# First attention: the third product of the turned scores folded into the second, with its operands built on ScalarE and VectorE

## The reference, cut to what matters

```python
q = (x @ Wq.T).reshape(B, T, NH, hd).transpose(0, 2, 1, 3)   # B=8 T=256 NH=16 hd=16
...
att = jnp.einsum('bhtd,bhsd->bhts', q, k) / jnp.sqrt(jnp.asarray(hd, x.dtype))
att = att + mask                      # causal
w = jax.nn.softmax(att, axis=-1)
z = jnp.einsum('bhts,bhsd->bhtd', w, v)
...
x = x + _layernorm(_L0_attn_ref(_layernorm(x, axis=-1), L0_attn_Wq, L0_attn_Wk, L0_attn_Wv, L0_attn_Wo), axis=-1)
```

## Time and profile before

| | |
|---|---|
| time, median of 3 runs | 1016.86 us (1005.52 to 1017.29) |
| the profiled execution's own time | 1014.95 us |
| its span in the trace | 1013.2 us |
| mean granted TensorE clock | 0.888 |
| PE busy | 853.5 us (84%), 6846 matmuls |
| PEld busy | 720.0 us (71%) |
| DVE busy | 741.6 us (73%) |
| ACT busy | 394.2 us (39%) |
| POOL busy | 441.6 us (44%) |

### The profile page before, as it was taken

How to read it: one execution, slowest core, us unless ns; L and a number is a source line. 1 busy time by engine, 2 the same in 40 slices (tenths; PEclk the granted TensorE clock), 3 DMA queues, 4 the chain that set the end, 5 groups by cost and what they waited for, 6 DMA issues and landing times. The chain is left out here.

```text
span 1013.2 us, 18850 instructions
## 1 busy us (share of the span) xinstructions
PE 853.5 (84%) x6846; PEld 720.0 (71%) x6846; DVE 741.6 (73%) x1561; ACT 394.2 (39%) x760; POOL 441.6 (44%) x582
## 2 busy tenths in 40 slices
PE   5899898897759877788888689999999989899973
PEld 4677777775648666677777568887878878788763
DVE  5678887876457653896666577888868777999894
ACT  2234333342323263333333254554455553333320
POOL 3123333322332237777775654666643213333332
PEclk9899999997669897899999977887778779999986
DMA  7000000000000037999987532211110000000001
GB/s 249 2 1 13 12 12 2 12 13 12 12 10 1 22 116 225 289 283 313 303 267 225 161 99 82 60 52 47 47 36 1 0 1 1 1 1 22 21 1 42
DMA packets 58315, 77.69 MB, mean 77 GB/s; under 512 B 9698, under 2 KB 50925, under 8 KB 58232
## 3 DMA queue, kind: packets, MB, share of 16 engines
q1 hardware_dynamic: 30968, 40.92, 12.8%
q0 software_dynamic: 9856, 18.92, 6.6%
q10 hardware_dynamic: 17408, 16.78, 4.8%
HBM read 61.88 MB, written 23.07 MB: 84 GB/s over the span
## 5 line engine op out<-in xcount | busy, mean ns | idle before, releaser
L516 POOL DMA_INDIRECT work<-xnd,rows_at x128 | 132.8, 1038 | 49.5 <-issue 33.2
L935 PE MATMUL ZO<-parts 128*128 128x256 f32 x288 | 90.6, 315 | 24.5 <-DVE parts L1523 7.2
L442 POOL TENSOR_SCALAR_AFFINE_SELECT work<-work 128x256 f32<-128x256 f32 x128 | 53.8, 444 | 128.4 <-ACT work L648 128.4
L433 POOL TENSOR_SCALAR veps<-mv 128x2 f32<-128x2 f32 x64 | 18.7, 292 | 193.3 <-DVE mv L1484 193.0
L1899 DVE TENSOR_TENSOR work<-work,S 64x256 f32<-64x256 f32 x128 | 54.2, 424 | 59.9 <-ACT work L774 55.8
L648 ACT ACTIVATE work<-S 128x768 f32<-128x768 f32 x64 | 52.0, 812 | 103.3 <-PE S L1008 103.3
L936 PE MATMUL ZO<-parts 128*128 128x256 f32 x288 | 84.9, 295 | 0.0
L937 PE MATMUL ZO<-parts 128*128 128x256 f32 x288 | 84.8, 294 | 0.0
L935 PEld LDWEIGHTS ZO<-parts 128*128 128x128 f32 x288 | 57.9, 201 | 33.1 <-issue 14.4
L935 PE MATMUL S<-xr,parts 128*128 128x512 f32 x192 | 79.2, 413 | 0.8 <-issue 0.8
L615 POOL TENSOR_TENSOR parts<-work,parts 128x512 fp32r<-128x512 f32 x32 | 44.1, 1378 | 80.3 <-ACT parts L891 80.3
(11 more groups left out here) (316 smaller groups left out, 2477.3 us busy)
## 6 DMA issues: line engine op xcount, KB each, us to landing
yd<-work ACTq DMA_DIRECT2D x64, 256.0 KB
raw<-in_experts SPq DMA_DIRECT2D x74, 192.0 KB
work<-in_experts SPq DMA_DIRECT2D x36, 192.0 KB
lg_all<-in_experts SPq DMA_DIRECT2D x18, 192.0 KB
raw<-in_ffn SPq DMA_DIRECT2D x2, 1536.0 KB, 7.4
xnd<-attn_w SPq DMA_DIRECT2D x8, 256.0 KB, 2.1
shd<-work SPq DMA_DIRECT2D x8, 256.0 KB, 2.4
work<-xnd,rows_at POOLq DMA_INDIRECT x128
```

Source lines behind the costliest of these rows:

```text
L442: last = pool.affine_select(out=diagonal, in_=diagonal, compare_op=ALU.is_ge, fill=0.0, base=0, pattern=[[0, 2], [1, P]], channel_multipli ...
L516: pool.indirect_dma_start(xg[:, i % RING, b, :], None, xnd[:], bass.IndirectOffsetOnAxis(ap=rows_at[:, 2 * i + b:2 * i + b + 1], axis=0), ...
L935: pe.matmul(dst, a(0), b(0), start=start, stop=False, skip_group_check=True)
```

## The change

Two of the three products become one. The key's low part needs only 16 of the 32 rows of a strip; the other 16 rows are now used for the selector of the maxima. So the second product's operands are `kx0`, which holds the key's low part in the upper 16 rows and the selector in the lower ones, and `qx0`, which holds `qm0` in the upper and the maxima's rows in the lower ones. A step has 8 turned matmuls instead of 12. To build the operands:

- ScalarE makes a third copy for each group, `khm`: the key times `upper` (1 in upper rows, 0 in lower) plus a negated selector. It stands ahead of the signal `a_q`.
- VectorE's second instruction in `key_copies` subtracts `khm` from the masked key; it is a scalar_tensor_tensor instead of a tensor_tensor.
- `spread_maxima` writes two copies of 32 elements each into `nmx` (zeros elsewhere) instead of one of 224.
- `maxima_low` has a second instruction, which waits for the first and forms `qx0` of group 0; a new `maxima_rows` forms groups 1 to 3 in one instruction of 768 elements, behind `key_copies(i+1, 1)`. `a_nm` is signalled twice in a round, and steps 0 and 2 of the turned scores wait for it.
- A few small instructions at the program's start build the masks.

```diff
             def query_copies(b, g):
                 act.wait_ge(s["a_qk"], 4 * b + g + 1)
                 act.activation(qh0, O[:, 0:T], ACT.Copy)
-                act.activation(kh0[:, b % 2, g, :], O[:, T:2 * T], ACT.Copy).then_inc(s["a_q"], 1)
+                act.activation(kh0[:, b % 2, g, :], O[:, T:2 * T], ACT.Copy)
+                act.activation(khm, O[:, T:2 * T], ACT.Identity, scale=upper[:, 0:1], bias=neg_pick[:, 0, g:g + 1]
+                               ).then_inc(s["a_q"], 1)
...
-                    side = (kh0, kl0)[k][rows, b % 2, g, half * P:(half + 1) * P] if k < 2 else                         bc(selc[rows, 2 * u + r:2 * u + r + 1], [32, P])
-                    top = (qm0[rows, b % 2, g, :] if k < 2 else nm0[rows, :])[:, half * P:T]
+                    side = (kh0, kx0)[k][rows, b % 2, g, half * P:(half + 1) * P]
+                    top = (qx0[rows, g, :] if k else qm0[rows, b % 2, g, :])[:, half * P:T]
...
-                    if u == 0:
-                        pe.wait_ge(s["a_nm"], b + 1)
+                    if u in (0, 2):
+                        pe.wait_ge(s["a_nm"], 2 * b + u // 2 + 1)
                     pe.wait_ge(s["a_exp"], 8 * b + u)
-                    for k in range(3):
+                    for k in range(2):
...
-                dve.tensor_tensor(kl0[:, b % 2, g, :], O[:, T:2 * T], kh0[:, b % 2, g, :], ALU.subtract
-                                  ).then_inc(s["a_k"], 1)
+                dve.scalar_tensor_tensor(kx0[:, b % 2, g, :], O[:, T:2 * T], upper[:, 0:1], khm, ALU.mult, ALU.subtract
+                                         ).then_inc(s["a_k"], 1)
...
-                dve.tensor_copy(nmx[:, :, H0:P].rearrange("p t (n h) -> p t n h", h=H0),
-                                bc(nmx[:, :, 0:H0].unsqueeze(2), [P, 2, 7, H0])).then_inc(s["a_nmx"], 1)
+                for t in range(2):
+                    last = dve.tensor_copy(nmx[:, t, :].rearrange("p (j c g) -> p j c g", c=8, g=4)[:, :, 4:6, :],
+                                           bc(best0[:, t, :].rearrange("p (g j) -> p j g", j=4).unsqueeze(2), [P, 4, 2, 4]))
+                last.then_inc(s["a_nmx"], 1)
...
-                dve.scalar_tensor_tensor(nm0, nmh, negm[:, 0:1], Z[:, 0:T], ALU.mult, ALU.add).then_inc(s["a_nm"], 1)
+                ch(dve.scalar_tensor_tensor(nm0, nmh, neg_low[:, 0:1], Z[:, 0:T], ALU.mult, ALU.add))
+                dve.scalar_tensor_tensor(qx0[:, 0, :], qm0[:, b % 2, 0, :], upper[:, 0:1], nm0, ALU.mult, ALU.add
+                                         ).then_inc(s["a_nm"], 1)
+
+            def maxima_rows(b):
+                dve.scalar_tensor_tensor(qx0[:, 1:4, :], qm0[:, b % 2, 1:4, :], upper[:, 0:1],
+                                         bc(nm0.unsqueeze(1), [P, 3, T]), ALU.mult, ALU.add).then_inc(s["a_nm"], 1)
...
                 if nxt:
                     key_copies(i + 1, 1)
+                if now:
+                    maxima_rows(i)
```

More of the change, by code:

```diff
@@ L85, in build @@
         negm = sb("negm", [P, 1])
+        upper = sb("upper", [P, 1])
+        neg_low = sb("neg_low", [P, 1])
+        neg_pick = sb("neg_pick", [P, 2, 4])
+        best0 = sb("best0", [P, 2, H0])
         onesr = sb("onesr", [P, 2, 2 * HD0])
@@ L182, in build @@
         qk_at = parts[:, NI * 2 * BW - 4096:]
-        qm0, kh0, kl0 = (parts[:, 8192 + i * 2048:10240 + i * 2048].rearrange("p (b g t) -> p b g t", b=2, g=4)
+        qm0, kh0, kx0 = (parts[:, 8192 + i * 2048:10240 + i * 2048].rearrange("p (b g t) -> p b g t", b=2, g=4)
                          for i in range(3))
-        qh0, nmh, nm0, selc = (parts[:, 14336 + i * T:14592 + i * T] for i in range(4))
+        qh0, nmh, nm0, khm = (parts[:, 14336 + i * T:14592 + i * T] for i in range(4))
+        qx0 = parts[:, 15360:16384].rearrange("p (g t) -> p g t", g=4)
         q1, k1 = (qk_at[:, 4096 + i * 1024:4096 + (i + 1) * 1024].rearrange("p (k g t) -> p k g t", k=2, g=2)
@@ L1005, in turned @@
                     rows = slice(32 * j, 32 * j + 32)
-                    side = (kh0, kl0)[k][rows, b % 2, g, half * P:(half + 1) * P] if k < 2 else                         bc(selc[rows, 2 * u + r:2 * u + r + 1], [32, P])
-                    top = (qm0[rows, b % 2, g, :] if k < 2 else nm0[rows, :])[:, half * P:T]
+                    side = (kh0, kx0)[k][rows, b % 2, g, half * P:(half + 1) * P]
+                    top = (qx0[rows, g, :] if k else qm0[rows, b % 2, g, :])[:, half * P:T]
                     return pe.matmul(S[2 + r][:, 2 * half * P:(2 + half) * P], side, top,
-                                     start=k == 0 and half == 0, stop=k == 2,
+                                     start=k == 0 and half == 0, stop=k == 1,
                                      skip_group_check=True)
@@ L1040, in values @@
                 if c and b + 1 < NB:
-                    pe.wait_ge(s["a_nm"], b + 2)
+                    pe.wait_ge(s["a_nm"], 2 * b + 3)
                 elif c:
@@ L1537, in maxima @@
                 dve.wait_ge(s["a_sc"], 8 * b + u + 1)
-                dve.tensor_reduce(nmx[:, 0, h:h + 2], pair[:, :, 0:P], AXX, ALU.max, negate=True)
-                dve.tensor_reduce(nmx[:, 1, h:h + 2], pair[:, :, P:3 * P], AXX, ALU.max, negate=True
+                dve.tensor_reduce(best0[:, 0, h:h + 2], pair[:, :, 0:P], AXX, ALU.max, negate=True)
+                dve.tensor_reduce(best0[:, 1, h:h + 2], pair[:, :, P:3 * P], AXX, ALU.max, negate=True
                                   ).then_inc(s["a_mx"], 1)
@@ L1640, in _ @@
             ch(dve.tensor_scalar(negm[:], negm[:], -1.0, None, ALU.mult))
-            ch(dve.tensor_reduce(rinv[:, 0:H0], ident[:].rearrange("p (n h) -> p h n", h=H0), AXX, ALU.add))
-            ch(dve.tensor_copy(selc[:, 0:H0], rinv[:, 0:H0]))
+            dve.tensor_scalar(upper[:], negm[:], 1.0, None, ALU.add)
+            strips = ident[:].rearrange("p (j c g) -> p j c g", c=8, g=4)
+            ch(dve.tensor_reduce(neg_low[:], strips[:, :, 5, :], mybir.AxisListType.XY, ALU.add))
+            dve.tensor_scalar(neg_low[:], neg_low[:], -1.0, None, ALU.mult)
+            for c in range(2):
+                last = dve.tensor_reduce(neg_pick[:, c, :], strips[:, :, 4 + c, :].rearrange("p j g -> p g j"), AXX,
+                                         ALU.add)
+            ch(last)
+            ch(dve.scalar_tensor_tensor(neg_pick[:, 0, :], neg_pick[:, 0, :], -1.0, neg_pick[:, 1, :], ALU.mult,
+                                        ALU.subtract))
+            dve.memset(nmx, 0.0)
             dve.wait_ge(s["x_in"], 16)
```

## The result

| | before | after |
|---|---|---|
| time, median | 1013.44 us (4 runs, 1005.52 to 1017.29) | 1033.94 us (4 runs, 1026.77 to 1041.96) |
| ratio | | 1.0215, 95% interval 1.0108 to 1.0321 |
| profiled execution: time, span | 1014.95, 1013.2 us | 1031.09, 1029.4 us |
| end of the first attention in the span | 298.4 us | 320.9 us |
| TensorE instructions (PE) | 6846 | 6590 |

The changed kernel is slower, by 20.5 us of the medians; the interval runs from 1.1 to 3.2%, so that it is slower is clear, and whether by more than 2% is not. The forecast was 1020 us and no measurable change, with 1008 to 1031 us as the range for 8 in 10; the time lies above it. 256 matmuls are gone, and the first attention ends 22.5 us later. (In the two profiled executions the second layer's attention, which is the same code, happened to take 7 us less in the changed kernel, so their spans differ by 16 us only.

The account below looks back on a forecast made before the run. A relay between TensorE and VectorE was taken to bound the kernel; terms before round 0 and in rounds 0 to 7 summed to +4.3 us on 1014.95, 1019.2, stated as 1020 us. Range for 8 in 10: 1008 to 1031.

Parts of the forecast that it names:

- The relay: Full round: TensorE hands over to VectorE six times, so only lengthened or shortened handovers count; +0.90 us a round; chance 0.6.
- TensorE's 17.9 us: Turned scores of the first attention: one product of 0.28 us less in each of 64 steps leaves TensorE.
- Each wait that I named: TensorE's waits on the router's and values' copies grow to 1.0 us or more; those on a group's operands grow too.
- the clock falls: Rival, rounds 1 to 6: longer TensorE idleness lowers its clock; 1031 us at one fall a round, 1043 at two; chance 0.2.
- the sum of +4.3 us: Whole first attention: +1.6 before round 0, +0.35 rounds 0 and 1, +3.6 rounds 2 to 5, +0.84 round 6, -2.1 round 7.
- some 2 us a fall: Clock rival's price for each fall, from two earlier windows in round 0 that lost 1.7 us of TensorE's work, plus longer waits.
- ScalarE's copy: Third copy per group, 32 in all, ahead of `a_q`: delays the signal 0.28 us; upper bound 0.41 us.
- hidden up to the reciprocal: Full round's start: VectorE's added 0.95, 0.52 and 0.06 us fit in its 1.92 us of idleness before `normalise`.
- the spread's two copies: VectorE's spread copy of 0.29 us becomes two taking 0.2; 0.08 us saved, between 0.15 saved and 0.1 lost.
- Before round 0: Five groups in sequence through TensorE, ScalarE and VectorE, each 0.28 + 0.06 us longer, less 0.08: +1.6 us.
- The 768-element instruction: VectorE's instruction for groups 1 to 3: 0.95 us, hidden before the reciprocal; rival of VectorE or ScalarE much dearer, chance 0.03.
- From round 7 to the end of the attention: Round 7: TensorE and ScalarE take turns, so every matmul less is gain; -2.1 us.

Follow-up runs that it names:

- both legs taken back: Changed kernel with low part and selector merged by GpSimd for groups 1 to 3, group 0 keeping three products, no second maxima instruction; ratio 1.0107.
- only a group's legs longer: Kernel before plus ScalarE's third copy per group, unread, ahead of `a_q`, and the slower second key copy on VectorE, 12 matmuls kept; ratio 1.0223.

## Why the prediction was wrong, step by step

Against the round's start, in us; the rows of before are the earlier trace rows:

| | before | forecast | after |
|---|---|---|---|
| turned scores of step 0 | 1.43 | +0.52 | +0.51 |
| values' products | 2.97 | +0.24 | +0.96 |
| reciprocal | 5.84 | +0.24 | +2.12 |
| group behind the values' copy | 10.13 | +0.24 | +2.12 |
| its L1522 (L1529) | 12.52 | +0.52 | +2.58 |
| group behind the router's copy | 16.94 | +0.58 | +2.43 |
| its L1522 (L1529) | 19.33 | +0.86 | +3.62 |
| transposes | 20.29 | +0.92 | +3.68 |
| next round | 30.44 | +0.90 | +3.74 |

- **The relay, and no gain from TensorE's 17.9 us: right.** With the product alone taken out, a full round is 0.2 us shorter, not 2.2. Each wait that I named grew, but for the one on the spread maxima (0.40 for 0.41). With the clock held, all legs cost 1.39 us a round where I had said 0.90.
- **The rival "the clock falls" was the case; weighing it at 2 in 10 was the error.** It is what failed: the sum of +4.3 us had no term for the clock, and the falls are 2.3 of the 3.7 us a full round. In rounds 0 to 6 together the change loses 21.3 us, and 13.2 of them come back with the waits filled (20.2 and 12.1 in the other traced execution). I saw that TensorE would be busy for 79% of a round and had the earlier trace rows of a fall behind a stretch of waits, but then let round 3's clock of 1.00 speak for the new round, whose waits were not those of before. Once or twice a round was right. Its price, "some 2 us a fall", was too high: measured are 0.70 us for the fall in the projection and 1.61 for the one in the values' products, 2.3 for both. At two falls a round I had 1043 us, and 1033.94 came.
- **ScalarE's copy: mis-sized.** 0.28 us expected, 0.46 measured (0.57 long); I took the row of an instruction without operands per partition. Twice in a full round, 0.36 us. My upper bound of 0.41 for its length was below the truth, so the range did not hold it either.
- **A wait overlooked.** In the round's start the transposes L914 (L921) wait for `key_copies`, which now stand behind the maxima's second instruction: 0.26 us. I had named what is queued behind that instruction on VectorE and taken it for hidden up to the reciprocal, without asking who else waits for it.
- **Small ones.** `next_input_low`'s subtraction took 0.68 instead of 0.89 us and gave 0.2 back; the spread's two copies save nothing (0.28 for 0.29). 0.90 + 0.36 + 0.26 - 0.21 + 0.07 = 1.38, and 1.39 were measured with the clock held.
- **Before round 0 and in round 0.** Round 0 starts 3.45 us later (forecast +1.6). The dearer copy on five legs is 0.9 of the difference; the rest was not taken apart, and with the same legs other executions start it 2.7 to 3.8 us later. It takes 2.96 us more (forecast +0.2), nearly all of it clock: with the waits filled it takes 26.37, 0.32 over before.
- **The 768-element instruction: right.** 1.01 us against 0.95, hidden. **From round 7 to the end of the attention: the number came, but by luck.** It is 54.0 against 56.3 us, -2.3 for a forecast of -2.1. But the changed kernel's other execution takes 56.3 us there at a clock of 0.62 (0.66 in the first), the kernel with both legs taken back 56.2, and the kernel with all 12 products and only a group's legs longer 54.1, at 0.69. The stretch's clock moves it as much as the products do, so their gain there is not shown.

The attention's 22.5 us are thus: 3.45 before round 0, 2.96 in it, 0.5 in round 1, 14.9 in rounds 2 to 5, 2.96 in round 6, less 2.3 from round 7 on.

## What to carry to other kernels

In a pipeline where TensorE hands over and waits, taking matmuls out brings what its waits let through, and adding an instruction ahead of a handover costs each time what it delays the signal: count the legs, not the busy time. Wherever a change lengthens TensorE's waits, work out the time at the lower clock as a case of its own with a real chance, even if the clock of the kernel before never moved there; filling the waits with unread matmuls tells the clock's part from the legs', but fill them in the kernel before too, or part of the gain is one that the old kernel could have had as well. Price an ACTIVATE by a row with the same operands.

## What the runs showed of the hardware that I had not expected

- TensorE's clock fell to its lower level in rounds in which no single wait of the engine is longer than 1.36 us, and in which it is busy for 83% of the time (28.26 of 34.18 us). With a longest wait of 1.33 us and 85% (both legs taken back) it held in all four full rounds. Small bf16 matmuls of 256 columns in the waits, five at a time, kept it at the upper level throughout rounds 0 to 5 of the changed kernel.
- The unread matmuls cost next to nothing where they fit: the kernel before with three ahead of each wait has a full round of 30.47 us instead of 30.45.
- An ACTIVATE over 128x256 from PSUM pays 0.07 to 0.09 us for each operand per partition, scale or bias: 0.39 or 0.40 without, 0.48 with one, 0.57 with both.
- GpSimd's tensor_scalar with two operands per partition over 128x256 in SBUF takes 1.27 us. Beside it the full round still takes 30.25 us; GpSimd has the room. The kernel with both legs taken back, 100 to 240 us:

```profile
L455 POOL TENSOR_SCALAR parts<-parts,upper,neg_pick 128x256 fp32r<-128x256 f32 x14 | 17.8, 1271 | 0.0
```
